# Two sets of four PSUM banks for even and odd steps, with TensorE doing two first stages and then two second stages

## The reference: what is computed

```python
def _gn(v, G=32, eps=1e-5):                 # groups of 12 channels, per image
    ...
    return ((g - m) / jnp.sqrt(s + eps)).reshape(v.shape)

# each of the 48 positions: 8 channels, one rounded shift and one fraction
disp = _displace(x.reshape(B, P, cpp, h, w), off_int)
# a 5x5 kernel that is a product of a row part and a column part
kernel = jnp.exp(-jnp.sum(d * d, axis=-1) / (2.0 * SIGMA ** 2))
kernel = kernel / jnp.sum(kernel, axis=(1, 2), keepdims=True)
out = lax.conv_general_dilated(disp, kw, ..., feature_group_count=C)
x = x + _L0_conv_ref(_gn(x), L0_conv_offset)
```

## Time and profile before

| | |
|---|---|
| time, median of 3 runs | 1280.02 us (1278.77 to 1281.33) |
| the profiled execution's own time | 1280.09 us |
| its span, first to last instruction | 1278.3 us |
| TensorE (PE) busy | 1200.4 us, 94% |
| VectorE (DVE) busy | 990.3 us, 77% |
| ScalarE (ACT) busy | 708.4 us, 55% |
| GpSimd (POOL) busy | 658.1 us, 51% |
| moved to and from HBM | 403.06 MB, mean 315 GB/s |
| mean granted TensorE clock | 0.994 |

### The profile page before, as it was taken

The page is one execution under the profiler, slowest core; times in us unless marked ns, Lnnn a source line. Parts: engine busy times, 40 slices in busy tenths (PEclk is TensorE's granted clock), DMA queues, the critical chain, the costliest instruction groups (busy, mean ns, idle before and its releaser), DMA issues.

```text
span 1278.3 us, 110940 instructions
## 1 busy us (share of the span) xinstructions
PE 1200.4 (94%) x49408; PEld 1140.1 (89%) x49408; DVE 990.3 (77%) x1530; ACT 708.4 (55%) x595; POOL 658.1 (51%) x1478
## 2 busy tenths in 40 slices
PE   2899999999999999999999999999999999999995
PEld 2799999999999999999999999999999999999995
DVE  5788787778778778787778778778787788778862
ACT  3464655656555565655646555565555656555552
POOL 4645545554554645545554554645545554554540
PEclk9899999999999999999999999999999999999998
DMA  9699999999999999999999999999999999999854
GB/s 314 218 327 332 320 333 329 331 326 325 323 334 329 324 329 331 327 323 335 319 332 331 324 317 340 330 324 331 319 336 317 335 325 324 332 328 326 290 169 151
DMA packets 409768, 403.06 MB, mean 315 GB/s; under 512 B 16528, under 2 KB 409744, under 8 KB 409744
## 3 DMA queue, kind: packets, MB, share of 16 engines
q1 hardware_dynamic: 204944, 201.41, 48.9%
q10 hardware_dynamic: 204800, 201.36, 47.3%
HBM read 201.38 MB, written 201.33 MB: 315 GB/s over the span
## 4 chain that ended last, share of the span: by engine, by line
PE 81%; ACT 13%; issue 4%; DVE 1%; POOL 1%; ACTq 0%; POOLq 0%; DVEq 0%
PE yp L608 59%; PE xp L617 18%; ACT y L555 13%; PE xp L600 3%; DVE stats L440 0%; ACTq L554 0%; DVE xin L462 0%; POOL t_int L231 0%; POOL t_full L237 0%; POOL grid_i L211 0%; POOL var L280 0%; POOL rstd L282 0%; POOL norm L293 0%; DVE both L447 0%; DVE sub L378 0%
## 5 line engine op out<-in xcount | busy, mean ns | idle before, releaser
L608 PE MATMUL yp<-ay,norm 32*128 32x128 f32 x24576 | 762.3, 275 | 45.2 <-ACT y L555 35.3
L608 PEld LDWEIGHTS yp<-ay,norm 32*128 32x128 f32 x24576 | 716.9, 188 | 65.1 <-issue 50.7
L555 ACT ACTIVATE y<-yp 128x1536 f32<-128x1536 f32 x256 | 371.5, 1451 | 467.5 <-PE yp L608 467.5
L440 DVE BATCH_NORM_STATS2 stats<-xin 128x6 f32<-128x512 f32 x768 | 509.4, 692 | 0.1
L617 PE MATMUL xp<-ax,y 64*64 64x64 f32 x24576 | 420.8, 221 | 5.9 <-issue 4.6
L617 PEld LDWEIGHTS xp<-ax,y 64*64 64x64 f32 x24576 | 384.7, 135 | 37.4 <-issue 6.9
L459 DVE TENSOR_TENSOR xin<-xp,xin 128x512 f32<-128x512 f32 x256 | 176.9, 691 | 252.6 <-PE xp L617 251.1
L293 POOL TENSOR_SCALAR norm<-xin,rstd,bias 128x768 f32<-128x768 f32 x256 | 252.4, 986 | 201.3 <-PE yp L608 166.2
L462 DVE TENSOR_TENSOR xin<-xp,xin 128x1024 f32<-128x1024 f32 x256 | 309.2, 1208 | 7.1 <-PE xp L617 7.1
L546 ACT ACTIVATE norm<-xin,bias,rstd 128x768 f32<-128x768 f32 x256 | 261.7, 1023 | 58.5 <-issue 42.8
L273 POOL TENSOR_TENSOR mean_sq<-both 128x4 f32<-128x4 f32 x128 | 25.5, 199 | 269.4 <-DVE both L447 267.4
(11 more groups left out here) (54 smaller groups left out, 191.0 us busy)
## 6 DMA issues: line engine op xcount, KB each, us to landing
xin<-in_x_dram SPq DMA_DIRECT2D x512, 384.0 KB, 5.3
out_dram<-xin ACTq DMA_DIRECT2D x512, 384.0 KB, 4.3
off<-in_L_conv_offset_dram SPq DMA_DIRECT2D x1, 48.0 KB, 3.2
```

The lines of the kernel that those rows point to most:

```text
L440: nc.vector.bn_stats(stats[:, s // PAIR % RING, s % PAIR, n, :], xin[:, s].rearrange("p (g q) f -> p q f g", g=GROUPS)[:, n]).then_inc(bn_ ...
L555: nc.scalar.activation(y[:, v].rearrange("p k r a m -> p a (k r) m"), yp[:, :, 0:POS * P].rearrange("p a (n m) -> p a n m", m=32), ACT.Cop ...
L608: last = nc.tensor.matmul(yp[:, a, P * k:P * (k + 1)], norm[rows, v, r, P * k:P * (k + 1)], ay[rows, k, r, :], start=(r == 0), stop=(r == ...
```

## The change

PSUM becomes one tensor of two sets of four banks. Even steps use set 0 and odd steps set 1. The second stage of a step writes its result over the first stage's result in the same set, once ScalarE has copied that to `y`. The sums of the statistics stand in set 0 beyond the columns of the first stage. TensorE's order for a pair becomes y(even), y(odd), x(even), sums, x(odd). ScalarE and GpSimd normalise a step two steps ahead, right after the first stage that used that buffer, and ScalarE does it after `copy_y` and the store. VectorE does the adds of its own step first, and the statistics of two steps in one go at each odd step, `AHEAD` is 8, `swap_rows` moves to `s == 14`, ahead of the adds, and `swap_columns` to after the adds of `s == 15`. Parts of the next superblock's matrices move by one to four steps. The first pair of steps is inside TensorE's loop, and the statistics sums of both first pairs come ahead of the first y.

```diff
-AHEAD = PAIR * (LEAD + 1)
+AHEAD = PAIR * (LEAD + 2)
-        yp = ctx.enter_context(nc.psum_tensor("yp", [P, LANES, 512], F32))
-        xp = ctx.enter_context(nc.psum_tensor("xp", [P, 4, 2, ROW], F32))
+        ps = ctx.enter_context(nc.psum_tensor("ps", [P, 2, LANES, 512], F32))
+        SUMS = slice(POS * P, POS * P + PAIR * GROUPS * 9)
-        SPARE = 2
+        SPARE = 1
...
# GpSimd, before the steps, and in step(c, s)
-            normalise(0, 0, 0, first=True)
+            for s in range(PAIR):
+                normalise(s, s, 0, first=True)
             column_matrices(0)
             make_summands(1, 1, early=True)
+            coefficients(1, 1, early=True, used=False)
-                if not (tail and s == STEPS - 1):
-                    normalise(t + 1, ...)
+                if not (tail and s + PAIR >= STEPS):
+                    normalise(t + PAIR, ...)
-                    if s == 2:   ->  s == 3    whole_distances(c + 1)
-                    if s == 4:   ->  s == 5    full_distances(c + 1)
-                    if s == 10:  ->  s == 12   column_matrices(c + 1)
...
# VectorE, before the steps
+            all_statistics(3)
             swap_columns(0)
             swap_rows(0)
-            all_statistics(3)
             sums(1, 1, early=True)
-            all_statistics(4)
-            all_statistics(5)
+            for s in range(2 * PAIR, AHEAD):
+                all_statistics(s)
# VectorE, step(c, s), new
+                if s == STEPS - PAIR and not tail:
+                    swap_rows(c + 1)
+                for part in range(ADDS):
+                    add_x(t, s, part)
+                if s % PAIR == 0:
+                    if not (tail and s // PAIR + LEAD >= STEPS // PAIR):
+                        sums(p + LEAD, (s // PAIR + LEAD) % 2, read=True)
+                else:
+                    if s == STEPS - 1 and not tail:
+                        swap_columns(c + 1)
+                    if not (tail and s + AHEAD >= STEPS):
+                        for f in (s - 1 + AHEAD, s + AHEAD):
+                            statistics(..., 0, ...)
+                            statistics(..., 1)
+                            statistics(..., 2)
+                    if s == 11 and not tail:
+                        values(c + 1)
...
# ScalarE, step(c, s)
-                if not (tail and s == STEPS - 1):
-                    normalise(t + 1, ...)
                 copy_y(t, s % 2, head and s <= 1)
                 if s >= BEHIND:
                     store(c, s - BEHIND, t - BEHIND)
                 elif not head:
                     store(c - 1, s - BEHIND + STEPS, t - BEHIND)
+                if not (tail and s + PAIR >= STEPS):
+                    normalise(t + PAIR, ...)
-  square at s == 4 and 6, exponential at 7, fill_rows at 10 and 11
+  square at s == 5 and 7, exponential at 9, both fill_rows at 13
...
# TensorE, two_steps
                 y_product(2, 0)
-                if not head:
-                    pe.wait_ge(result0_ready, one)
-                    x_products(1, one)
-                    if more:
-                        pe.wait_ge(summands_ready, one)
-                        pe.wait_ge(result0_ready, two)
-                        sum_stats()
-                pe.wait_ge(y_ready, one)
+                pe.wait_ge(result0_ready, one)
+                pe.wait_ge(result1_ready, one)
                 pe.wait_ge(norm0_ready, two)
                 y_product(0, 1)
                 pe.wait_ge(norm1_ready, two)
                 y_product(1, 1)
                 y_product(2, 1)
...
-                if more:
-                    pe.wait_ge(sums_ready, one)
-                pe.wait_ge(ax_ready, one)
-                pe.wait_ge(result0_ready, two)
-                x_products(0, two)
-                if not last:
-                    begin_y(three, two)
+                pe.wait_ge(ax_ready, one)
+                pe.wait_ge(y_ready, one)
+                pe.sem_inc(x_started, 1)
+                x_products(0)
+                if more:
+                    pe.wait_ge(summands_ready, one)
+                    pe.wait_ge(result0_ready, two)
+                    sum_stats()
+                pe.wait_ge(y_ready, two)
+                pe.sem_inc(x_started, 1)
+                x_products(1)
+                if not last:
+                    pe.wait_ge(result0_ready, two)
+                    pe.wait_ge(result1_ready, two)
+                    if more:
+                        pe.wait_ge(sums_ready, one)
+                    begin_even(three)
```

More of the change, by code:

```diff
@@ L510, in _ @@
             run(step)
-            for part in range(ADDS):
-                add_x(TOTAL - 1, STEPS - 1, part)
         @block.scalar
@@ L564, in _ @@
                 fill_rows(0, part)
-            normalise(0, 0, 0, True)
+            for s in range(PAIR):
+                normalise(s, s, 0, True)
             def store(c, s, t):
@@ L574, in step @@
                 t = STEPS * c + s
-                if not (tail and s == STEPS - 1):
-                    normalise(t + 1, (s + 1) % STEPS, STEPS // PAIR * c + (s + 1) // PAIR, head and s == 0)
                 copy_y(t, s % 2, head and s <= 1)
@@ L581, in step @@
                     store(c - 1, s - BEHIND + STEPS, t - BEHIND)
+                if not (tail and s + PAIR >= STEPS):
+                    normalise(t + PAIR, (s + PAIR) % STEPS, STEPS // PAIR * c + (s + PAIR) // PAIR, False)
                 if not tail:
-                    if s == 4:
+                    if s == 5:
                         square(c + 1, 0)
-                    if s == 6:
+                    if s == 7:
                         square(c + 1, 1)
-                    if s == 7:
+                    if s == 9:
                         exponential(c + 1)
-                    if 10 <= s < 10 + B:
-                        fill_rows(c + 1, s - 10)
+                    if s == 13:
+                        for part in range(B):
+                            fill_rows(c + 1, part)
             run(step)
@@ L611, in y_product, with x_products, begin_even @@
                     last.then_inc(y_done, 1)
[L613 to L634 removed]
+            def x_products(v):
+                for k in (2, 0, 1):
+                    for r in range(R):
+                        for h, m in ((0, 0), (1, 0), (0, 1), (1, 1)):
+                            rows, outs = slice(64 * h, 64 * h + 64), slice(64 * m, 64 * m + 64)
+                            at = ROW * (k % 2) + HW * r
+                            last = nc.tensor.matmul(ps[outs, v, 2 * (k // 2) + h, at:at + HW],
+                                                    y[rows, v, k, r].rearrange("p a m -> p (a m)")[:, outs], ax[rows, k],
+                                                    start=True, stop=True)
+                    if k > 0:
+                        last.then_inc(x_done, 1)
+            def begin_even(number):
                 pe.wait_ge(norm0_ready, number)
@@ L637, in begin_y, with two_steps @@
                 y_product(0, 0)
-            def two_steps(one, head=False, more=True, last=False):
+            def two_steps(one, more=True, last=False):
                 two, three = one + 1, one + 2
@@ L678, in _ @@
             sum_stats()
-            begin_y(1, None)
-            two_steps(1, head=True)
-            with pe.Fori(PAIR + 1, PAIR * (PAIRS - LEAD) + 1, PAIR) as one:
+            pe.wait_ge(first_sums, 1)
+            pe.wait_ge(first_summands, 2)
+            sum_stats()
+            pe.wait_ge(first_sums, 2)
+            begin_even(1)
+            with pe.Fori(1, PAIR * (PAIRS - LEAD) + 1, PAIR) as one:
                 two_steps(one)
```

75 lines of the change are left out of this document (14 added, 61 removed).

## The result

The changed kernel takes 1217.86 us (median of 4 runs, 1216.96 to 1218.91) against 1280.55 beside it: a ratio of 0.9513, 95% interval 0.9496 to 0.9529. The profiled execution has a span of 1215.1 us, and the forecast for the span was 1232.9.

A forecast was written before the change was run, and what follows sets the result against it. TensorE was taken to set the pace, interrupted by waits for ScalarE's copy of y. Start 45.9, 124 pairs x 9.26 (1148.2), swaps 8 and end 30.8 gave a 1232.9 us span, forecast 1235 us, range 1222 to 1262.

The forecast's parts named there:

- What bounds the kernel, and the wait that goes: TensorE sets the pace; its wait for ScalarE's copy of y goes, a gain of 0.34 us a pair.
- the later one: Between x(even) and x(odd), the later of sums or ScalarE's copy of the odd y sets the term, 1.92 us.
- two transitions do not occur before, and I take the start-to-start values: TensorE's y to y and unwaited x to y: taken from nearest rows, 2.89 and 1.56 us; ends -0.06 and +0.14 a pair.
- after that nothing is waited for: TensorE's start: after the first y at about 25.2 us no waits, third y at 36.6, fifth at 45.9.
- The swap: Row matrices swapped ahead of step 14's adds: sums wait 0.54 us once a superblock, 15 times, +8 us.
- The new waits ahead of the even y: TensorE waits for both even-step adds and the sums read; done at 3.00 against 3.48, about 0.3 us spare.
- ScalarE's queue: Copy, two stores and normalise of the even y precede the odd y's copy; 0.1 us spare, costed at nothing.
- Rival A: ScalarE's copy of the odd y comes late, by 0.1 to 0.3 us a pair: 1247 to 1272; chance 0.12 with some gain.
- rival B: VectorE's add, reduction and release before the even y take longer than 3.48 us; 1260 us, chance 0.05.
- The end: Last two pairs, outside the loop: two at 9.26, 6.5 of issue waits, last add 1.2, then 4.6; 30.8 us.
- Rival C: DMAs fall behind and VectorE's statistics wait for loads, holding up the adds; at 320 GB/s 1306 us, chance 0.05.
- The estimate by which 341 GB/s would be the most: DMA limit from the skill's table for 1 MB transfers: a pair would need 9.23 us and nothing would be spare.

The follow-up runs named there:

- Half the copy: Against the changed kernel, ScalarE copies only two of the four lanes of the first stage's result in odd steps; 1217.37 us.
- The runs with a round between: Changed kernel plus four small matmuls inside the odd first stage: 1276.78 us with the second stage's tile shape, 1244.57 with the first stage's.

## Why the prediction was wrong, step by step

**What bounds the kernel, and the wait that goes.** Right. The wait of y for ScalarE's copy is gone, 33.7 us in 121 times before, none after. The terms for x, for x with the sums (1.91, forecast 1.92) and for x(odd) (1.56) are right to 0.01 us. Half the copy shows that the sums set the 1.91 now, as "the later one" of two that end together.

**The step that failed: two transitions do not occur before, and I take the start-to-start values.** I gave y to y the 2.89 us that is y to x, with 0.06 below it as the lower end. Two y take 5.59, so the second adds only 2.70: 0.19 less, three times beyond my bound. I had named the reason, a y to y without a change of tile shape, and gave it a few hundredths without a row for them. The runs with a round between show that a passage from one tile shape to another costs 0.15 us one way and 0.21 the other, 0.18 on the average, and the new order has four where the old had five. Over 124 pairs the 0.19 us are 24 us, more than the whole miss of 17.8, and more than half again on top of the 0.34 us that I counted for the wait. The pairs were shorter by only 21.6 us in all, since about 3 us came back where the y after x(odd) starts late. The trace of before held a hint: inside a first stage the 24 rounds of four start 0.112 us apart, 2.7 us in all, while from one stage's start to the next are 2.89, with a passage in it.

**The start: after that nothing is waited for.** Wrong. The first y was forecast at 25.2 and came at 24.79. The fifth was forecast at 45.9, with 50 as its later bound, and came at 52.46: two waits for issue, 4.5 us, and slow stages about them (the third and fourth y took 7.0 us for 5.6, at a granted clock of 0.69 between 40 and 44 us, a mean of stretches at 2.4 and at 1.2 GHz). Against the forecast the waits are 4.5 us, the second stages and sums between the second and the third y another 2.3, and the third and fourth y 1.1; the first y began 0.4 earlier and the first two y were 0.9 shorter. In the kernel before, the first pair's code was straight and TensorE stood waiting for summands anyway, so these waits had no row of their own. The Trainium skill, "Runtime: NRT & Kernel Launch", Instruction fetch mechanics, says that code comes in blocks of 16 KiB by a DMA queue of the sequencer and that TensorE's memory for it holds 2048 instructions, more than the loop has; the trace agrees: packets of 16384 bytes on q8, and these, like the waits for issue of over 0.4 us, only at the first pass of the loop and in the code behind it.

**The swap.** Right: 0.54 forecast, 0.50 measured, 7.4 us in 15 waits (7.0 in the 14 that name the add), and 7.0 us come back when it is moved.

**The new waits ahead of the even y, and ScalarE's queue.** Right: no wait is named there, apart from the 0.04 us and more in a quarter of the pairs. The 0.1 us spare of ScalarE's queue was all used up, since y(odd) ends 0.19 earlier than I counted, and even so it was late by only 0.02 and cost nothing. Rival A and rival B did not come.

**The end.** Forecast 30.8, measured 28.1: the waits for issue were 3.3 us and not 6.5. I had taken them over unchanged. The rest of the end was 0.5 us longer than forecast.

**Rival C, the DMAs.** Refuted: 344 GB/s in the middle, and the statistics wait 0.1 us in all. Stores take 6.2 us to land and not 4.3, inside the slack. The estimate by which 341 GB/s would be the most is passed.

## What to carry to other kernels

Where TensorE changes between stages of different tile shape, count the passages in each order as work, at the price that a row of the trace shows for one, and group stages of one shape before looking for idle time. A stage's own time is to be taken from inside the stage; the distance between the starts of two different stages has a passage in it. If a buffer is doubled, ask which order it permits: here the order made the gain, and the two sets of banks without it, each result written over its input, lost 31%.

## What was not expected of the hardware

A passage from 32x128 to 64x64 tiles cost 0.15 us and one back 0.21, where nothing was waited for. The first pass through TensorE's loop cost two waits for issue, 2.0 and 2.5 us, each over 1.3 us after a packet of 16384 bytes on q8 had landed. The first went when fewer loads were in flight. The second stayed, 2.7 to 4.2 us in the experiments with this order: about 2.4 us of it are the packet and the time behind it, and what sets the rest stays open.
